# Transformer and expert kernel on one core: scatter of expert group 14 brought forward, returned rows of token group 0 reduced tile by tile, two base sums placed later

## What is computed

```python
x = _layernorm(x + _L0_attn_ref(x, ...))      # causal linear attention, 16 heads
x = _layernorm(x + _L0_ffn_ref(x, ...))       # 64 experts, the best 8 of each token, plus a shared expert
x = _layernorm(x + _L1_attn_ref(x, ...))      # 4 encoder layers of linear attention and a feed-forward part
x = _layernorm(x + _L1_ffn_ref(x, ...))       # a router chooses 192 of 256 tokens for a gelu block

def _L0_ffn_ref(...):
    shared_out = _swiglu(x, shared_w1, shared_w2)
    ...                                        # each token's 8 experts and their weights
    out = einsum(x1 * silu(x2), expert_w2)     # per expert, up to 160 tokens
    y = out[se, rank] * sw                     # weighted result rows
    combined = zeros((T, H)).at[st].add(y)     # sum of a token's 8 rows
    return shared_out + combined
```

## Time and profile before

| | us |
|---|---|
| median of 3 runs | 718.93 |
| lowest, highest | 718.65, 720.97 |
| the profiled execution | 723.01 |
| its span in the profile | 721.2 |

### The profile page before, as it was taken

The page is one execution under the profiler, slowest core; times in us unless marked ns, Lnnn a source line. Parts: engine busy times, 40 slices in busy tenths (PEclk is TensorE's granted clock), DMA queues, the critical chain, the costliest instruction groups (busy, mean ns, idle before and its releaser), DMA issues.

```text
span 721.2 us, 11097 instructions
## 1 busy us (share of the span) xinstructions
PE 580.0 (80%) x3755; PEld 479.8 (67%) x3755; DVE 453.1 (63%) x1362; ACT 230.2 (32%) x434; POOL 345.1 (48%) x341
## 2 busy tenths in 40 slices
PE   7998878668987787797999035789999999999960
PEld 5767655668977776797995024567787778778640
DVE  4678768943424322333433787887877787777994
ACT  3142234002322212222332011224344444443664
POOL 4656101873566666576444488343322332342352
PEclk9999997879999999999999556799999999999995
DMA  8960001126666766676716900000000000000001
GB/s 298 415 260 23 16 7 36 45 72 203 209 222 200 231 220 190 190 237 218 239 61 213 398 2 0 0 12 5 15 26 4 15 15 11 4 30 0 1 1 59
DMA packets 29564, 79.42 MB, mean 110 GB/s; under 512 B 7104, under 2 KB 12096, under 8 KB 29264
## 3 DMA queue, kind: packets, MB, share of 16 engines
q1 hardware_dynamic: 23088, 65.69, 26.3%
q0 software_dynamic: 6432, 13.16, 6.0%
HBM read 62.60 MB, written 16.25 MB: 109 GB/s over the span
## 4 chain that ended last, share of the span: by engine, by line
PE 58%; DVE 23%; issue 8%; another core or an unknown queue 4%; POOL 2%; ACT 2%; DMA 1%; SPq 0%; DVEq 0%; ACTq 0%; POOLq 0%
PE bank L780 13%; PE bank L946 6%; PE bank L790 6%; PE bank L934 6%; PE bank L539 4%; PE bank L876 3%; PE bank L894 2%; DVE stats L256 2%; DVE arena L1659 2%; PE bank L857 2%; PE bank L871 2%; DVE hidden L1743 2%; PE bank L885 2%; PE bank L912 2%
## 5 line engine op out<-in xcount | busy, mean ns | idle before, releaser
L271 POOL TENSOR_TENSOR rstd<-veps,minus_half 128x4 f32<-128x4 f32 x52 | 54.0, 1039 | 209.9 <-DVE veps L264 208.4
L780 PE MATMUL bank<-hidden,ring 128*128 128x160 f32 x768 | 123.4, 311 | 4.6 <-issue 2.7
L780 PEld LDWEIGHTS bank<-hidden,ring 128*128 128x128 f32 x768 | 113.4, 200 | 6.5 <-issue 4.3
L1347 POOL DMA_INDIRECT returned_rows<-x1t,scatter_all x80 | 79.3, 991 | 65.9 <-DVE x1t L1754 21.8
L1153 ACT ACTIVATE hidden<-bank 128x480 f32<-128x480 f32 x64 | 36.9, 576 | 177.6 <-PE bank L780 110.5
L790 PE MATMUL bank<-hidden,ring 128*128 128x160 f32 x384 | 66.4, 310 | 31.8 <-DVE hidden L1743 19.1
L790 PEld LDWEIGHTS bank<-hidden,ring 128*128 128x128 f32 x384 | 56.0, 193 | 37.3 <-DVE hidden L1743 22.8
L1731 DVE COPY hidden<-bank 128x384 f32<-128x384 f32 (+1 forms) x32 | 22.9, 719 | 66.3 <-PE bank L780 33.9
L1211 ACT ACTIVATE arena<-bank,layer_cols 128x512 f32<-128x512 f32 x64 | 44.0, 687 | 62.6 <-PE bank L934 62.6
L946 PE MATMUL bank<-ring,arena 128*128 128x128 f32 x512 | 59.9, 275 | 1.4 <-issue 1.4
L946 PEld LDWEIGHTS bank<-ring,arena 128*128 128x128 f32 x512 | 58.4, 192 | 2.4 <-issue 2.4
(11 more groups left out here) (222 smaller groups left out, 1156.9 us busy)
## 6 DMA issues: line engine op xcount, KB each, us to landing
ring<-in_ew SPq DMA_DIRECT2D x64, 576.0 KB
returned_rows<-zeros SPq DMA_DIRECT2D x16, 512.0 KB, 14.6
arena<-returned_rows SPq DMA_DIRECT2D x6, 512.0 KB, 12.7
hidden<-returned_rows SPq DMA_DIRECT2D x4, 512.0 KB, 5.0
ring<-returned_rows SPq DMA_DIRECT2D x4, 512.0 KB, 8.6
ring<-in_l1w SPq DMA_DIRECT2D x8, 256.0 KB, 2.6
returned_rows<-x1t,scatter_all POOLq DMA_INDIRECT x80
shared<-in_xr SPq DMA_DIRECT2D x1, 1024.0 KB, 8.3
```

Source lines behind the costliest of these rows:

```text
L271: pool.tensor_tensor(rstd[:, s, :], veps[:, s, :], minus_half[:], ALU.pow).then_inc(sem(f"rstd{which}_ready"), 1)
L780: mm = pe.matmul(bank[2 * (n % 2) + part][:, CAP * f:CAP * f + CAP], ring[:, n % RING, P * (FB * part + f):P * (FB * part + f) + P], E["xt ...
L1347: pool.indirect_dma_start(returned_dram[:, :], bass.IndirectOffsetOnAxis(ap=scatter_all[:, Q, b:b + 1], axis=0), E["back"][:, Q % BACK, b, ...
```

## The change

Five edits, with the lines of the diff that carry them.

1. On PE, `turn_results(14, 0)` moves from before `expert_hidden(63)` to behind `expert_hidden(62)`, and `turn_results(14, 1)` takes its place before `expert_hidden(63)`. It was behind `expert_result(62)`. DVE's `rows_back(14, ...)` moves with them, and POOL's two `step` waits fall away for groups 14 and 15.
2. The four tiles of token group 0 count on a semaphore each (`returned_tile0` to `3`). Names of other semaphores are merged in pairs, since their number is limited; their waits count 16 higher.
3. `SUMMED = (4, 2, 0, 0)`: all of group 0 is summed on DVE, and for every tile that DVE sums one `tensor_reduce` over the 8 rows takes the place of the three halvings. It reads 1,024 numbers of a partition and writes 128; the 8 numbers of one sum lie 128 numbers (512 bytes) apart.
4. `add_base(2)` and `add_base(3)` move behind `collect(0)` and behind the first item's `norm_stats`. The late products 10 and 11 move behind the small constants. PE's first `project` gets a wait for all four base sums, since it writes bank 4.
5. The wait of `collect(g)` for POOL's sums is left out where POOL has no tile.

```diff
-        SUMMED = (3, 2, 0, 0)
+        SUMMED = (4, 2, 0, 0)
+        def returned_in(i):
+            return sem(f"returned_tile{i}") if i < GT else sem(f"returned_in{i // GT}")
...
             for i in range(TILES):
-                sp.dma_start(spare[i], mine[i]).then_inc(sem(f"returned_in{i // GT}"), 16)
+                sp.dma_start(spare[i], mine[i]).then_inc(returned_in(i), 16)
...
                 elif j == 3 and Q >= 1:
-                    turn_results(Q - 1, 0)
+                    turn_results(Q - 1, 0 if Q < NEG - 1 else 1)
                 pe.wait_ge(sem(f"expert_in{n % RING}"), 16 * (n // RING + 1))
-                expert_hidden(n).then_inc(sem("expert_mm"), 1)
-            expert_result(NE - 2)
-            turn_results(NEG - 2, 1).then_inc(sem("expert_mm"), 1)
+                done = expert_hidden(n)
+                if n == NE - 2:
+                    done = turn_results(NEG - 2, 0)
+                done.then_inc(sem("expert_mm"), 1)
+            expert_result(NE - 2).then_inc(sem("expert_mm"), 1)
...
+                if k == 0:
+                    pe.wait_ge(sem("base_ready"), GROUPS)
...
             for Q in range(NEG):
                 n = EG * Q + 2 * EG
-                step(n)
+                if Q < NEG - 2:
+                    step(n)
...
-                step(n + 1)
+                if Q < NEG - 2:
+                    step(n + 1)
...
             def sum_tiles(g):
+                if SUMMED[g] == GT:
+                    return
...
-                elif j == 3 and Q >= 1:
+                elif j == 3 and 1 <= Q < NEG - 1:
                     rows_back(Q - 1, 0)
+                elif j >= 2 and Q == NEG - 1:
+                    rows_back(NEG - 2, j - 2)
                 product(n)
...
-            v.wait_ge(sem("expert_mm"), NE + 1)
-            rows_back(NEG - 2, 1)
...
-            add_base(SOON)
-            for m in range(FB * SOON + 4, FB * GROUPS):
-                late_product(m)
-            add_base(SOON + 1)
...
             def collect(g):
-                v.wait_ge(sem(f"returned_in{g}"), 16 * GT)
-                count = SUMMED[g]
-                if count:
-                    rows = spare_rows(g, 0, count)
-                    for width in (4 * D, 2 * D):
-                        ch.after(ch.did(v.tensor_tensor(rows[:, :, 0:width], rows[:, :, 0:width],
-                                                        rows[:, :, width:2 * width], ALU.add)))
-                    k = ch.did(v.tensor_tensor(H[:, g, 0:count, :], rows[:, :, 0:D], rows[:, :, D:2 * D], ALU.add))
+                if g:
+                    v.wait_ge(sem(f"returned_in{g}"), 16 * GT)
+                for t in range(SUMMED[g]):
+                    if g == 0:
+                        v.wait_ge(returned_in(t), 16)
+                    k = ch.did(v.tensor_reduce(H[:, g, t, :], spare[GT * g + t].rearrange("p (k d) -> p d k", d=D), AX.X,
+                                               ALU.add))
...
+                if k == -1:
+                    add_base(SOON + 1)
...
+                if k == -2:
+                    add_base(SOON)
...
+            for m in range(FB * SOON + 4, FB * GROUPS):
+                late_product(m)
```

More of the change, by code:

```diff
@@ L324, in program @@
         spare += [gates[:].rearrange("p i e -> p (i e)"), logits[:].rearrange("p i e -> p (i e)")]
-        SUMMED = (3, 2, 0, 0)
-        def spare_rows(g, first, count):
-            whole = (flat_hidden, flat_ring[:, at_spare:])[g]
-            return whole[:, TOPK * D * first:TOPK * D * (first + count)].rearrange("p (t n) -> p t n", t=count)
+        SUMMED = (4, 2, 0, 0)
+        def returned_in(i):
+            return sem(f"returned_tile{i}") if i < GT else sem(f"returned_in{i // GT}")
         own_s, place_s, chosen_m = (small[:, 800 + 16 * k:816 + 16 * k] for k in range(3))
@@ L495, in project_first @@
                 if g == 1:
-                    pe.wait_ge(sem("second_xt_in"), 16)
+                    pe.wait_ge(sem("second_xt_then_qkv_in"), 16)
                 if g == 2:
-                    pe.wait_ge(sem("xt_in"), 16)
+                    pe.wait_ge(sem("xt_then_up_in"), 16)
                 if g:
@@ L589, in attention_out @@
                 if g == 0:
-                    pe.wait_ge(sem("wo_in"), 16)
+                    pe.wait_ge(sem("wo_then_o_in"), 16)
                 pe.wait_ge(sem("an_ready"), g + 1)
@@ L614, in route_logits @@
                 if g == 0:
-                    pe.wait_ge(sem("sw_in"), 16)
+                    pe.wait_ge(sem("sw_then_down_in"), 16)
                 pe.wait_ge(sem("x1t_ready"), g + 1)
@@ L904, in output @@
             def output(n, k, g, l):
-                pe.wait_ge(sem("o_in"), 16 * (l + 1))
+                pe.wait_ge(sem("wo_then_o_in"), 16 * (l + 2))
                 pe.wait_ge(sem("at_ready"), n + 1)
@@ L924, in up @@
             def up(n, k, g, l):
-                pe.wait_ge(sem("up_in"), 16 * (l + 1))
+                pe.wait_ge(sem("xt_then_up_in"), 16 * (l + 2))
                 pe.wait_ge(sem("h2t_ready"), n + 1)
@@ L937, in down @@
             def down(n, k, g, l):
-                pe.wait_ge(sem("down_in"), 16 * (l + 1))
+                pe.wait_ge(sem("sw_then_down_in"), 16 * (l + 2))
                 pe.wait_ge(sem("relu_ready"), FFB * (n + 1))
@@ L1810, in collect @@
             def collect(g):
-                v.wait_ge(sem(f"returned_in{g}"), 16 * GT)
-                count = SUMMED[g]
-                if count:
-                    rows = spare_rows(g, 0, count)
-                    for width in (4 * D, 2 * D):
-                        ch.after(ch.did(v.tensor_tensor(rows[:, :, 0:width], rows[:, :, 0:width],
-                                                        rows[:, :, width:2 * width], ALU.add)))
-                    k = ch.did(v.tensor_tensor(H[:, g, 0:count, :], rows[:, :, 0:D], rows[:, :, D:2 * D], ALU.add))
+                if g:
[5 more added lines that the diff above has]
+                                               ALU.add))
+                if SUMMED[g]:
                     ch.after(k)
-                v.wait_ge(sem("pool_sums"), 3 * sum(GT - n for n in SUMMED[:g + 1]))
+                if SUMMED[g] < GT:
+                    v.wait_ge(sem("pool_sums"), 3 * sum(GT - n for n in SUMMED[:g + 1]))
                 v.wait_ge(sem("base_ready"), g + 1)
```

26 lines of the change are left out of this document (13 added, 13 removed).

## The result

The changed kernel takes **723.39 us** (median of 20 runs, 719.50 to 726.04), the kernel before, run beside it, 719.60 (20 runs). The ratio is 1.0048, interval 1.0033 to 1.0064: slower by 3.5 us (0.0048 x 719.6; the two medians lie 3.8 apart), where 2.9 us less were forecast. The profiled execution took 724.27 us with a span of 722.5.

A forecast was written before the change was run, and what follows sets the result against it. Near the change, group 0's data and DVE's own work ended together, and everything to the first layer hung on DVE. Gains of 1.6 + 1.3 = 2.9 us took 718.93 to 716.0 us, range 713.0 to 718.2.

The forecast's parts named there:

- Part 1: Group 14 turned earlier: all ten scatters 2.25 us earlier, PE's steps 0.4 us later, nothing gained for group 0.
- slower case: Rival for DVE's reductions: 3.3 us each, base add of group 0 4.3 us late, 723.2 us in all; chance 0.04.
- Part 2: DVE free earlier for group 0's sum: only late products stand ahead, ending at 394.65 us; data no longer bind.
- Part 3: Price of one strided reduction on DVE, 1.82 us; four end at 401.6, group 0's base add 1.6 us earlier.
- dense rate: Rival for DVE's reductions: the stride costs nothing, 1.22 us each, 713.6 us in all; chance 0.22.
- heavy stride: Rival for DVE's reductions: 2.30 us each, only group 1 gains, 717.9 us in all; chance 0.19 together with contention.
- three steps a number: The stride rate assumed in the slower case: 3.1 ns a number, 3.3 us a reduction on DVE; chance 0.04.
- Part 4: Base sums on DVE, 0.69 us each, fit where DVE idled 1.15 and 1.12 us; uncovered they would cost 0.7 each.
- Part 5: Group 1's sums on POOL: adds not slowed by DVE's reductions, two tiles in 5.2 us, 1.3 us gained.
- Sum: Whole kernel: 1.6 us from group 0 and 1.3 from group 1, 2.9 us less, 716.0 us.

The follow-up runs named there:

- e5: The changed kernel, but POOL keeps its two step waits for groups 14 and 15; ratio 0.9948 to the kernel before.
- e3: The changed kernel with group 14's turns, rows and step waits as before, all other edits kept; ratio 0.9959 to the kernel before.
- e8: e3 with the two base sums and the last two late products back in their old places; ratio 1.0030 to the kernel before.
- e6: The changed kernel without the new turns of group 14 on PE and DVE, POOL's two step waits still dropped; ratio 0.9965 to the kernel before.
- e11: e5 with group 0 summed in two pairs of tiles by dense adds; ratio 0.9936 where the kernel before takes 677.89 us.
- e13: The changed kernel run again, unaltered, on a chip where the kernel before takes 678.20 us; ratio 0.9946.

## Why the prediction was wrong

- **Part 1 is the step that failed**, in the sentence "The price is on PE: two more transposes stand ahead of expert 63's hidden product, 0.38 us, and every step from there, the late half too, comes 0.4 us later." The transposes cost nothing in the end: e5, which has them, reaches `turn_late` after 8.41 us, before 8.50. What I left out was on another engine. The scatters that start 2.25 us earlier close the gap of 2.56 us on POOL, and with that gap gone the signal of expert 63 reached DVE and ACT 4.3 us late: 5.6 us on PE's chain, 0.5 more by its clock. I had read the gap as a loss. On the chips at 720 us the next signal came on time only with it.
- That all ten scatters come 2.25 us earlier fell with it: the first does (372.89 - 368.77 = 4.12 us behind expert 62, before 6.38), the last starts at 389.16. That part 1 buys nothing for group 0 held: in e3 the returns start at the old distance, 20.51 us behind expert 62 (before 20.43), and its four reductions still wait for no tile. So a part that I had costed at no gain carried the whole risk, and it had no rival in which it costs time: my slower case was the stride, with 0.04.
- That slower case gave 723.2 us, and 723.39 was measured. The agreement is chance: it rests on a reduction of 3.3 us, and one takes 1.91.
- **Part 2** was right in form: the reductions stand right behind the last late product. Forecast 24.8 us behind expert 62, e5 24.25; the changed kernel has 30.35 only through part 1.
- **Part 3**: four reductions in 7.41 us against 4 x 1.82 - 0.3 = 7.0. One takes 1.91 us, (1.912 - 0.153) / 1.024 = 1.72 ns a number, between the two strided rows, 1.63 and 1.77. The dense rate, the heavy stride and the three steps a number are all out. The Trainium skill (VectorE: DVE Perf Modes, The perf-mode tier table and Mode 1×) says that this mode takes any stride and names no price for one; read as no price, it gives the dense 1.22 us, an estimate, and the row does not agree.
- **Part 4**: the base sums hide: DVE still idles 0.63 us behind the first (forecast 0.4) and 0.53 behind the second. e8 puts 4.1 us on their place.
- **Part 5**: POOL's two tiles take 3.98 + 0.87 us for 5.39 + 0.87, 1.4 us less where 1.3 was forecast. The rule of the Trainium skill (SBUF — State Buffer, Who interferes with whom), that `tensor_reduce` on this chip never takes the port pair that VectorE shares with GpSimd, agrees with this: 1.27 us for an add beside a reduction, 1.94 beside DVE's adds.
- **Sum**: -2.9 us was forecast; e3, without part 1, has -3.0, and e5, with part 1 and its gap, -3.7 by the ratio and 46.20 - 49.51 = -3.3 by the profile. The changed kernel's +3.5 is +2.8 at the base add of group 1; the rest lies within the interval (2.4 to 4.6 us).

Open stays why TensorE's signal is held. A long run of POOL's indirect transfers is part of it on the chips at 720 us, not sufficient there, and without effect on those at 678. Whether a met wait would do in place of a pause wasn't settled either: it ran only where there is nothing to cure.

The best version is the changed kernel with POOL's waits kept (e5). It has the lowest ratio of those tried at 720 us (0.9948; the intervals of e3 and e6 overlap with its own), and with the pairs (e11) it is 0.9936 at 678, where it didn't run without them.

## What to carry to other kernels

A gap on an engine that isn't the bound can be what lets another one through: before a transfer is moved into it, look in the same trace for what happens to other engines' signals where that queue has no gap, and give that case a chance of its own. Parts that are forecast to bring nothing are best left out, or tried alone, for they can still cost. And where two chips give a kernel different times, the sign of a change measured on one of them need not hold on the other.

## What the runs showed of the hardware

On the chips where before takes 720 us such late signals are common: the trace of before has 25 idle times of 3 us or more on DVE from 157 to 338 us, in the expert stage. By its semaphore records, 15 of the 51 raises of `expert_mm` that they hold from 150 to 345 us come over 1 us behind the end of the matmul that raises it; in e13 it is none of 66. The first count is rough, since some matmul records of that trace can be missing. DVE in the kernel before, and POOL beside it:

```profile
242.58 0.42 DVE L1754 TENSOR_TENSOR x1t<-bank,slot_gate 128x256 f32<-128x256 f32 x1 [5.10 <-PE bank L780]
```

```profile
241.45 0.95 POOL L1340 DMA_INDIRECT logits<-dispatch_rows,gather_all  x1 [0.30 <-issue]
243.35 1.01 POOL L1347 DMA_INDIRECT returned_rows<-x1t,scatter_all  x1 [0.95 <-PE bank L780]
```

DVE goes on when POOL's transfer has ended, and in ten of the 25 places it does so 2.3 to 2.6 us behind the start of POOL's last transfer, as at expert 63 (375.46 and 377.89). This alone shows no cause, since POOL waits in its `step` for the same signals. A part of it could have been read ahead of the run: the earlier trace rows put 26.0 us of idle time in front of L1731 down to "remote". In e13 two such idle times are left in that stage. The busy times from 180 to 260 us, first before, then e13:

```profile
180.00:260.00 80.00, 66.66 (x467) 63.80 (x466) 26.84 (x54) 19.92 (x44) 50.66 (x52) 0.98 0.67 216
```

```profile
180.00:260.00 80.00, 80.00 (x606) 80.00 (x604) 38.17 (x76) 27.21 (x59) 61.12 (x63) 1.00 0.90 281
```

PE does 606 matmuls in place of 467 in the same 80 us and never stops, and the transfers move 281 GB/s for 216. Expert 62's hidden product starts at 369.81 us in before and at 322.86 in e13, 47 us earlier, and the spans differ by 48.5: the chips differ in the stages up to there, by ten times what this change is about. Behind the base add of group 1 the changed kernel takes 301.4 us on the one and 672.7 - 370.64 = 302.1 on the other. The granted clock (0.98 and 1.00) is not the reason.
